# Scores and look-ahead of an attention kernel as 64 by 64 tiles of the TensorE array

## The reference, cut to what matters

```
x: (2, 64, 96, 96) fp32, B = 2, C = 64, N = 96*96 = 9216
h = group_norm(x);  f = dwconv3(h) + dwconv5(h) + dwconv7(h)
x = x + conv1x1(f * sigmoid(conv1x1(f, gate)), proj)
h = group_norm(x);  q, k, v = conv1x1(h, ...)            # each C x N
attn = softmax(q^T k * C**-0.5, axis=-1)                 # N x N per batch
out = x + (attn @ v)^T
```

## Time and profile before

| | us |
|---|---|
| median of 3 runs | 2857.21 (2855.27 to 2861.93) |
| the profiled execution | 2859.16 |
| its span in the profile | 2857.2 |
| PE busy | 2766.2 (97%) |
| DVE busy | 2519.7 (88%) |
| ACT busy | 2223.1 (78%) |
| POOL busy | 1824.8 (64%) |

### The profile page before, as it was taken

How to read it: one execution, slowest core, us unless ns; L and a number is a source line. 1 busy time by engine, 2 the same in 40 slices (tenths; PEclk the granted TensorE clock), 3 DMA queues, 4 the chain that set the end, 5 groups by cost and what they waited for, 6 DMA issues and landing times.

```text
span 2857.2 us, 54567 instructions
## 1 busy us (share of the span) xinstructions
PE 2766.2 (97%) x19644; PEld 941.4 (33%) x19644; DVE 2519.7 (88%) x3183; ACT 2223.1 (78%) x2338; POOL 1824.8 (64%) x1479
## 2 busy tenths in 40 slices
PE   6689999999999999999988999999999999999998
PEld 4333333333333333333323333333333333333332
DVE  4489999999999999999767999999999999999994
ACT  4267888888888888888866788888888888888887
POOL 1246666666666666666664666666666666666666
PEclk9899999999999999999998999999999999999999
DMA  7402000000000000000001000000000000000000
GB/s 192 115 8 41 10 10 10 10 10 10 10 10 10 10 11 10 10 10 8 5 9 44 8 11 10 10 10 10 10 10 10 10 10 10 11 10 10 9 6 5
DMA packets 36089, 52.93 MB, mean 19 GB/s; under 512 B 7912, under 2 KB 34024, under 8 KB 35056
## 3 DMA queue, kind: packets, MB, share of 16 engines
q1 hardware_dynamic: 35824, 49.47, 7.1%
HBM read 21.13 MB, written 14.16 MB: 12 GB/s over the span
## 4 chain that ended last, share of the span: by engine, by line
PE 87%; DVE 8%; issue 3%; ACT 1%; DMA 0%; POOL 0%; POOLq 0%; SPq 0%; DVEq 0%; ACTq 0%
PE ps L944 39%; PE ps L935 32%; PE ps L951 11%; DVE mxp L757 4%; PE ps L1051 2%; DVE arena L780 1%; DVE ps L770 1%; PE ps L967 1%; ACT arena L529 0%; DVE ps L773 0%; DVE bn L856 0%; DVE arena L866 0%; DVE x_max L857 0%; PE ps L1028 0%; DMA QM<-arena 0%
## 5 line engine op out<-in xcount | busy, mean ns | idle before, releaser
L459 POOL TENSOR_TENSOR arena<-arena 128x512 f32<-128x512 f32 x1224 | 1558.3, 1273 | 799.2 <-ACT arena L529 720.3
L757 DVE TENSOR_REDUCE mxp<-ps 128x1 f32<-128x1024 f32 x1296 | 1575.9, 1220 | 172.3 <-PE ps L951 141.7
L529 ACT ACTIVATE arena<-ps,bnd 128x1024 f32<-128x1024 f32 x1296 | 1373.9, 1111 | 412.6 <-PE ps L935 389.6
L944 PE MATMUL ps<-arena 128*64 128x512 f32 x5184 | 1268.1, 605 | 1.0 <-ACT pvb L539 1.0
L935 PE MATMUL ps<-arena 64*128 64x512 f16 x7776 | 1055.1, 377 | 5.0 <-ACT ps L566 3.2
L773 DVE TENSOR_TENSOR ps<-ps,arena 128x512 f32<-128x512 f32 x1260 | 870.2, 691 | 72.4 <-ACT arena L529 71.1
L566 ACT ACTIVATE ps<-mseed 128x1024 f32<-128x1024 f32 x612 | 629.1, 1028 | 53.3 <-ACT arena L529 0.4
L951 PE MATMUL ps<-arena,QM 64*128 64x512 f16 x2592 | 500.9, 383 | 18.9 <-DVE mxp L757 10.3
L935 PEld LDWEIGHTS ps<-arena 64*128 64x128 f16 x7776 | 375.1, 94 | 424.1 <-issue 31.8
L944 PEld LDWEIGHTS ps<-arena 128*64 128x64 f32 x5184 | 310.8, 136 | 505.2 <-issue 349.5
L951 PEld LDWEIGHTS ps<-arena,QM 64*128 64x128 f16 x2592 | 124.7, 93 | 735.8 <-DVE mxp L757 632.5
(11 more groups left out here) (110 smaller groups left out, 692.4 us busy)
## 6 DMA issues: line engine op xcount, KB each, us to landing
arena<-arena SPq DMA_DIRECT2D x144, 64.0 KB, 2.0
arena<-in_x_rows SPq DMA_DIRECT2D x8, 816.0 KB, 10.0
xs<-in_x SPq DMA_DIRECT2D x4, 1152.0 KB, 15.5
f_scratch<-arena SPq DMA_DIRECT2D x32, 144.0 KB
f<-f_scratch SPq DMA_DIRECT2D x16, 288.0 KB, 8.2
x_scratch<-arena SPq DMA_DIRECT2D x4, 1152.0 KB, 13.6
QM<-arena SPq DMA_DIRECT2D x72, 64.0 KB, 2.0
xst<-x_scratch SPq DMA_DIRECT2D x72, 64.0 KB, 2.2
```

What stands on the lines that cost most here:

```text
L459: nc.gpsimd.tensor_tensor(accA[:, n % 2, :], accA[:, n % 2, :], e, ALU.add).then_inc(adda_free, 1)
L529: nc.scalar.activation(flat(E[:, slot_of(n % 2, p), :, :]), flat(ps[:, S_BANK + 2 * buf:S_BANK + 2 * buf + 2, :]), ACT.Exp, scale=bnd[:, 6 ...
L757: nc.vector.reduce_max(flat(mxp[:])[:, v:v + 1], flat(ps[:, bank:bank + 2, :]), AX.X).then_inc(mx_free, 1)
L944: a = nc.tensor.matmul(ps[C * t:C * t + C, ACC_BANK, :], V[:, t, p, :], E[:, slot_of(par, p), t, :], start=(p == 0), stop=(p == NPAIR - 1) ...
```

## The change

Each score matmul and each look matmul of 64 rows by 128 columns becomes two of 64 rows by 64 columns, one for the first 64 keys (or queries) of the tile, which writes partitions 0 to 63 of the bank, and one for the other 64, which writes partitions 64 to 127. The banks, the terms, the waits, the semaphores (one increment on the last matmul) and the order of all other work stay as they are.

```diff
                 for k, (of, part) in enumerate(terms):
                     for t in (0, 1):
                         rows = slice(C * t, C * t + C)
-                        a = nc.tensor.matmul(ps[:, S_BANK + 2 * (p % 2) + t, :], of[rows], QS[rows, par, part, :],
-                                             start=(k == 0 and seeds is None), stop=(k == len(terms) - 1),
-                                             skip_group_check=True)
+                        for half in (0, 1):
+                            at = slice(C * half, C * half + C)
+                            a = nc.tensor.matmul(ps[at, S_BANK + 2 * (p % 2) + t, :], of[rows, at], QS[rows, par, part, :],
+                                                 start=(k == 0 and seeds is None), stop=(k == len(terms) - 1),
+                                                 skip_group_check=True)
                 a.then_inc(s_ready, 1)
...
             def max_scores(half, qt, kc, m, bank=MX_BANK):
                 for t in (0, 1):
                     rows = slice(C * t, C * t + C)
-                    a = nc.tensor.matmul(ps[:, bank + t, :], QM[rows, half, qt * P:(qt + 1) * P],
-                                         KH[rows, kc * CH:(kc + 1) * CH], start=True, stop=True)
+                    for side in (0, 1):
+                        a = nc.tensor.matmul(ps[C * side:C * side + C, bank + t, :],
+                                             QM[rows, half, qt * P + C * side:qt * P + C * side + C],
+                                             KH[rows, kc * CH:(kc + 1) * CH], start=True, stop=True)
                 a.then_inc(mx_ready, 1)
```

## The result

The changed kernel takes 2878.32 us (median, 2877.29 to 2880.26); the kernel before took 2857.52 in the same comparison. The ratio is 1.0074, 95% interval 1.0058 to 1.0090: slower by 0.74%, 20.8 us. The forecast was 2874, +17.

What follows compares the result with a forecast made beforehand. PE was taken to bound the kernel, in one stretch together with the loop look, reduction, look; 28 ns a cycle gave 15.3 us, plus 0.8 and 1, so +17 us on 2857.2: 2874, range 2853 to 2912.

Steps and rivals of the forecast that it cites:

- Nothing inside the rounds: In PE's rounds of 0.22 us: the 11,736 added matmuls and as many weight loads cost nothing, hidden by streaming.
- The exposed load: First look after a change of shape: its unhidden weight load costs 24 ns in place of 11, so +13 ns.
- The spread of starts: Ends of rounds: with four matmuls, three gaps of 4 ns make 12 in place of 4, so +8 ns.
- The first look 21 ns later: First look of a cycle: ends 13 + 8 = 21 ns later, which DVE and PE's next round hand on.
- The second look +7: Second look, whose loads wait for DVE: last matmul starts at 36 ns after the first load, not 29.
- The cycle: One attention cycle on PE: the three small terms sum to 28 ns, upper bound 100 ns.
- The 1 us for the stages ahead of the attention: Stages before the attention: 144 looks made between 128 by 128 products were given 1 us.
- Three cycles of a block bound by DVE: Around the end of a block: DVE has more to do, so these three cycles lose only about 10 ns each.
- The cheaper switch: Rival, switch into weigh and back: regrouping columns causes its 0.24 us, which would go, 122 us gained, 2735; chance 0.14.
- Dearer loads: Rival, ends of rounds: exposed load 51 ns, starts 7 ns apart, up to 100 ns a cycle, 2914; chance 0.14.
- Not sharing: Rival, inside rounds: tiles run one after the other, about 4100, or issue lengthens rounds, about 2980; chance 0.05.

Runs made afterwards that it cites:

- Eight products: Scores and looks as eight products of 64 rows by 32 columns, where the changed kernel has four of 64 by 64: 2900.09 us, ratio 1.0145.
- the short reduction: DVE's rough maximum reduces one look bank of two, 512 elements in place of 1024: 2840.09 us from the kernel before, 2852.22 from the changed one.
- the two half-way kernels: The changed kernel with only the looks put back to 64 by 128 (2986.39 us), or only the scores put back (2998.30 us).

## Why the prediction was right, step by step

The mechanism was right: nothing inside the rounds, a small cost at their ends, and part of it through DVE's loop. That the sum came so close is in part luck, since errors of both signs stood in it.

**Nothing inside the rounds: right.** Rounds are 0.22 us with two, four and eight products. The rows of weigh, the spread products and the convolution were the right evidence.

**The exposed load: right.** 24 ns was taken from the fp16 row, and 400 − 376 = 24 was measured. The Trainium skill, "TensorE: Matmul & The Clock Gate", LDWEIGHTS, gives columns / 1.2 GHz; by the 53 ns that follow from it, an estimate, the first look would have lasted 429, and the trace disagrees.

**The spread of starts: too large.** Three gaps were put at 12 ns, and the matmuls of a look start 10 ns apart from first to last. But only +3 of the +8 arrived: from first load to last matmul the first look went from 8 to 11 ns, because its first matmul now starts sooner after its load.

**The first look 21 ns later: too small, this is the term that was off.** Its reduction starts 26 ns later after the first load: 3 for the starts, 13 for the load, and 10 for the longer tail, a price per product that I had not put into the sum. Eight products confirm it: the time from load to reduction grows by 19 ns more, 14 for the starts and 19 for the tail, less 14 for the load. It acts only because DVE waits for this semaphore; with the short reduction the tail is still 53 ns and costs nothing.

**The second look +7: 5 measured, but put together otherwise.** I had the last matmul start 7 ns later after the first load, at 36. It starts 11 sooner (20 against 31), and its exposed load then makes it 16 longer. First load to weigh's first load went from 335 ns (31 + 304) to 340 (20 + 320).

**The cycle.** 28 forecast, 33 measured: 26 + 5 and 2 of rounding and DVE's wake-up. A block was forecast 0.45 us longer and is 0.55, which makes 3.5 us over 34 blocks, most of what separates +17 from +20.8. The 1 us for the stages ahead of the attention had no row behind it, and it speaks of 144 looks where there are 72 of two matmuls each; the two traces show no such loss ahead of the first attention.

**Three cycles of a block bound by DVE: wrong.** I read the distances of 2.41 and 1.96 us as DVE's work. The 2.41 is a plain 2.18 with the spread products inside, the 1.96 a stretch with a ninth round, because a pair there is not seeded. With the reduction halved the block should have become 0.8 us shorter, and it became 0.06.

In the stretch behind those rows DVE does hold PE back: from the look at 766.30 to the one at 768.27 there are eight rounds, 1.73, but it takes 1.97. The weight load of that look waits for the reduction:

```profile
768.27 0.10 PEld L951 LDWEIGHTS ps<-arena,QM 64*128 64x128 f16 x2 [0.57 <-DVE mxp L757]
```

With the short reduction this stretch takes 1.73 again (758.10 to 759.83). But one cycle later the scores come late, where the wait was 0.37 before:

```profile
763.38 0.36 PEld L935 LDWEIGHTS ps<-arena 64*128 64x128 f16 x6 [0.61 <-issue]
```

From the first of these looks to the fourth it is 5.96 us in both (766.30 to 772.26, 758.10 to 764.06), and 5.96 in the changed kernel too (770.97 to 776.93). In all three ACT ends its second seeding (line 566) 5.17 or 5.18 us after the first of these looks, and the late scores are loaded 0.11 later. So a chain through ACT seems to bound these two cycles and to cover what DVE or the looks lose there; no run isolates it.

Medians over the blocks of the two traces give the cost of each of the 18 cycles: 14 lose 33 or 34 ns, the one with the spread products 43, the one with the ninth round 18, the next two together 24. That is 0.55 us, where 15 × 28 + 3 × 10 was 0.45. The misreading cost little, because the cycles around the end of a block lose less for other reasons than mine. That was luck.

**The rivals.** The cheaper switch is refuted, for rows by the changed kernel itself (320 ns into weigh, of which 16 belong to the exposed second look, leaves the 304 of before) and for columns by the two half-way kernels. Dearer loads: the load was as forecast. Not sharing: refuted. What had spoken for the forecast was that the trace before has a place for each kind of regrouping by itself.

Left open: whether a wide load costs only 11 ns exposed because of how it is read. Exposed loads measured here are 11 ns for 128 columns of fp16, 24 for 64, 10 for 32, 51 for 64 of fp32. The Trainium skill, "TensorEngine Tiling (Array Packing)", Restrictions and Gotchas, has column tiling exclude Fast Weight Load, and a 128-column load cheaper than a 64-column one fits that; no run isolates it.

None of these runs points to a version that beats both kernels: the two that are faster leave half of the keys out of the maximum.

## What to carry to other kernels

Splitting these products into up to eight smaller tiles was free in the stream and paid for at its ends: with the load that is exposed after a change of shape, and with some 5 ns per product until a waiting engine may start. Keep neighbours in one tile shape, rows and columns both; each change cost about 0.1 us and the next load here, whichever of the two changed. To price such an edit, look in the trace for that kind of transition by itself, and for the engine that waits on the last product, since nearly half of this loss went through a loop with VectorE.

## What the runs showed of the hardware that I had not expected

Eight matmuls and eight weight loads go through in 215 ns, 27 ns for a matmul with its load, about what the convolution's row has (29), and the round does not grow. An instruction stream of that density stood still for 7.8 us while DMAs of 2.3 MB ran, and the next packet on PE's instruction queue started only as they ended; the granted clock was 0.50 for some 3 us afterwards. With the DMAs spread over four blocks the stall was gone. And a narrow weight load is not the cheaper one: 24 ns exposed for 64 columns against 11 for 128, though 10 for 32.
